# Attention maxima carried within SBUF, split in four operations, with another order at the start of each attention pair

## Chip, cores and metric

One core of one Trainium2 chip runs the whole program. The metric is the device time of one execution in microseconds, the median of several runs. Times inside an execution come from one profiled execution and count from its span's start.

## The reference

Four sequences of 512 tokens, 128 wide, go through six residual layers. Two are half-weighted attention over routed feed-forward projections (`_L0_ffn_ref`), two half-weighted mixtures of experts, one a state-space layer. The change touches only the causal multi-head attention between the two feed-forward layers:

```
q, k = rope(x @ wq.T), rope(x @ wk.T)           # 16 heads of 8
v    = x @ wv.T
scores = einsum('bhqd,bhkd->bhqk', q, k) / sqrt(8)
scores = scores + slopes[h] * (key position - query position)
scores = where(later key, -1e9, scores)
out = softmax(scores) @ v                       # softmax over keys
x = x + out @ out_w.T + out_b
```

## The kernel before

Everything is kept in SBUF; one program with five instruction streams (TensorE, VectorE, ScalarE, GpSimd and the DMA queue SP) that meet at semaphores. The sequences go in two pairs; each pair runs all six layers, and a layer's two sequences are two units. The attention of a pair is thus two units, one behind the other with a common plan, and stands at 131 to 250 us for the first pair and at 777 to 896 us for the second.

**What an attention unit does.** The 16 heads are four quads of four. In a first pass TensorE makes all scores in the order query by key ("slots", L1828 with the mask L1830, 11 slots to a quad, 44 to a unit), and VectorE reduces each to the negated row maximum (L1428). When the 11 slots of a quad are done, `max_parts` splits the float32 maxima into three bfloat16 parts. The job "turn" transposes these parts on TensorE to 12 rows (L1554, cbf with a_mp), ScalarE copies them to the tile a_mT (L1016), and SP brings them into three extra rows of each head's query operand a_qs, so that the maximum is subtracted within the product of the second pass. In that second pass TensorE makes the scores key by query (L1760, masks L1763 and L1765), ScalarE takes the exponential into a_p (L999), and TensorE weighs the values with it (L1789, `weigh_heads`).

**The plan.** The second pass has 32 steps for a unit (8 to a quad), 64 to a pair. `heads_plan()` writes the order of the other jobs by hand: the list at -1 runs before step 0, the others behind the scores of their step. The first unit's slots and turns go at 1.5 jobs a step until they are used up; `NEXT_MAXIMA` says in which steps the second unit's are taken; "vals" are the value projections, "rows" the transposes of finished heads, "ctr" and "out" the output projection. Step 8q of a unit waits for the maxima of quad q (L1754). All engines walk the same plan.

**Banks.** Jobs before number `RING_OF_4` (the length of the list at -1, less 3) use four PSUM banks in turn; later ones use two. `bank_free` makes TensorE wait for the reader of the job before in that bank, in the ring of two that of the second job before. The scores use the other banks.

**The next unit's preparation.** `hand_over(u, i)` runs stage i of the next unit: on VectorE 0 is the statistics of X (L1159 to L1178), 2 the Newton step (L1153 to L1155) and the normalised rows (L1188); the exponent guess of GpSimd stands between them (L773). Then follow the transposes, projections, rotations (L1405, L1409) and residuals (L1414) of queries and keys, and their bfloat16 parts by ScalarE (L906).

**SP's queue, in program order, for the first unit of a pair.** Quad 0: wait for a_mT, transfers. Quad 1: the same, then `head_rows(k + 1, 0)`, the second unit's query parts to stack_dram (L609, six transfers). Quad 2: wait for a_mT, transfers, then `head_rows(k + 1, 1)`, the key parts (L609, six). Quad 3: wait for step 15, `head_rows_in(k + 1, 0)` and `(k + 1, 1)`, which load a_q (L616) and a_k (L620) from stack_dram for the second unit's first slots; then wait for a_mT and transfers. Here "transfers" are one write of a_mT to max_dram (L708), a wait until it has landed, and two reads into a_qs (L712).

Of the kernel before, what the change touches and what calls it, by code (L numbers as in the profile page):

```python
# [8 lines left out]
BF16 = mybir.dt.bfloat16  # L9
# [4 lines left out]
P = 128  # L14
# [37 lines left out]
def heads_plan():  # L52


    def maxima(x):
        jobs = [("slot", x, n) for n in range(QUADS * NS1)]
        for quad in range(QUADS):

            jobs.insert((quad + 1) * NS1 + quad + 2, ("turn", x, quad))
        return jobs  # L60

    plan = {step: [] for step in range(-1, 2 * NS2 + 1)}
    first, second = maxima(0), maxima(1)
    plan[-1] = first[:NS1] + [("vals", 0, 0)] + first[NS1:NS1 + 8]
    first = first[NS1 + 8:]
    for step in range(2 * NS2):
        count = int(1.5 * (step + 1)) - int(1.5 * step)
        plan[step] += first[:count]
        first = first[count:]
        if step == NEXT_VALUES:  # L70
            plan[step].append(("vals", 1, 0))
        for start, stop, count in NEXT_MAXIMA:
            if start <= step < stop:
                number = int(count * (step + 1)) - int(count * step)
                plan[step] += second[:number]
                second = second[number:]
        x, quad = divmod(step // STEPS_4 - 1, QUADS)
        if step % STEPS_4 == 5 and step > STEPS_4:
            plan[step].append(("rows", x, quad))
        if step == NS2 + 7:  # L80
            plan[step].append(("ctr", 0, 0))
        if step == NS2 + 9:
            plan[step].append(("out", 0, 0))
    plan[2 * NS2] = [("rows", 1, QUADS - 1), ("ctr", 1, 0), ("out", 1, 0)]
    assert not first and not second
    return plan


NEXT_VALUES = 12
NEXT_MAXIMA = [(19, 51, 1.5)]  # L90
HEADS_PLAN = heads_plan()


# [80 lines left out]
def program(nc, A, out):  # L174
    with ExitStack() as ctx:
# [121 lines left out]
        a_o = sb("a_o", [P, T], F32, s)  # L297
        a_mx = sb("a_mx", [P, QUADS, NT, 4], F32, s)
        a_mr = sb("a_mr", [P, NT, 4], F32, s)
        a_mp = sb("a_mp", [P, QUADS, NT, 3, 4], BF16, s)  # L300
        a_rec = sb("a_rec", [P, NT, 4], F32, s)

        sb("f_end", [P, 352], F32, s)
# [45 lines left out]
        stack_dram = nc.dram_tensor("stack_dram", [2, 2, P // 2, HEADS // 2, T], BF16, kind="Internal").ap()  # L349
        comb_dram = nc.dram_tensor("comb_dram", [2, EXPERTS, T], F32, kind="Internal").ap()  # L350
        c_dram = nc.dram_tensor("c_dram", [2 * NSTATE, T], F32, kind="Internal").ap()
        max_dram = nc.dram_tensor("max_dram", [QUADS, 12, T], BF16, kind="Internal").ap()


        signals = []
# [93 lines left out]
        a_mpt = sig("a_mpt", "mha", QUADS)  # L449
        a_mtr = sig("a_mtr", "mha", QUADS)  # L450
        a_mok = sig("a_mok", "mha", QUADS)
        a_mwr = sig("a_mwr", "mha", QUADS, 16)
        a_mld = [sig(f"a_mld_{n}", "mha", 2, 16) for n in range(QUADS)]
        a_s2 = sig("a_s2", "mha", NS2)
        a_e2 = sig("a_e2", "mha", NS2)
        a_pv = sig("a_pv", "mha", 4 * NT)
# [128 lines left out]
        def _(sp):  # L585
# [104 lines left out]
            for u, (kind, p) in enumerate(UNITS):  # L690
                k = kth[u]
                if kind == "mha":
                    if p == 0:

                        sp.wait_ge(unit_done, done_before(u))
                        head_rows_in(k, 2)
                        head_rows_in(k, 3)
                    for quad in range(QUADS):
                        if p == 0 and quad == 3:

                            sp.wait_ge(a_s2.sem, a_s2.at(k, NS2 // 2 - 1))
                            head_rows_in(k + 1, 0)
                            head_rows_in(k + 1, 1)
                        sp.wait_ge(a_mok.sem, a_mok.at(k, quad))
                        if p == 1:

                            sp.wait_ge(a_mld[quad].sem, a_mld[quad].at(k - 1, 1))
                        a_mwr.by(sp.dma_start(max_dram[quad], a_mT))  # L708
                        sp.wait_ge(a_mwr.sem, a_mwr.at(k, quad))
                        for odd in range(2):  # L710
                            r = 64 * odd + MAX_ROW
                            a_mld[quad].by(sp.dma_start(a_qs[quad // 2][r:r + 3, 2 * (quad % 2):2 * (quad % 2) + 2],  # L712
                                                  max_dram[quad].rearrange("(c h o) t -> o c h t", c=3, o=2)[odd]))
                        if p == 0 and quad in (1, 2):
                            head_rows(k + 1, quad - 1)
                        if p == 0 and quad == QUADS - 1:

                            sp.wait_ge(a_s2.sem, a_s2.at(k, 3 * STEPS_4 - 1))
                            head_rows_in(k + 1, 2)
                        if p == 1 and quad == 0:  # L720

                            sp.wait_ge(a_s2.sem, a_s2.at(k - 1, NS2 - 1))
                            head_rows_in(k, 3)
                if kind == "ffn" and u + 1 < NU and UNITS[u + 1][0] == "mha":
                    k = kth[u + 1]
                    a_rld.by(sp.dma_start(rope[:], A["rope"]))
                    head_rows(k, 0)
                    if k == 0:
                        sp.wait_ge(rows_in, 64)
                        sp.wait_ge(w_lo.sem, w_lo.at(0, len(SPLITS) - 1))  # L730
                    head_rows(k, 1)
                    head_rows_in(k, 0)
                    head_rows_in(k, 1)
                if kind == "mamba":
                    state_rows(k)
                if u + 1 < NU and UNITS[u + 1][0] == "moe":
                    combine_rows(kth[u + 1], 1 - p)
                if kind == "moe" and u % PER_PAIR >= PER_PAIR - 2:
                    if p == 1:
                        for n in range(2):  # L740

                            sp.wait_ge(m_res.sem, m_res.at(k - 1 + n, 0))
                            b = batch_of(u - 1 + n)
                            load(out[b].rearrange("t p d -> p t d"), X[:, b], x_out)
# [104 lines left out]
        def _(act):  # L849
# [159 lines left out]
            def head_job(k, job, n):  # L1009
                b = job_bank(HEADS_JOBS.index((job, k % 2, n)))  # L1010
                if job == "turn":
                    act.wait_ge(a_mtr.sem, a_mtr.at(k, n))
                    if n >= 1 or k % 2 == 1:

                        act.wait_ge(a_mwr.sem, a_mwr.at(k, n - 1))
                    a_mok.by(act.activation(a_mT, bank[0:12, b, 0:T // 2].bitcast(BF16), ACT.Copy))  # L1016
                if job == "vals":
                    act.wait_ge(a_vpr.sem, a_vpr.at(k, 0))
                    if k % 2 == 1:

                        act.wait_ge(a_vok.sem, a_vok.at(k - 1, 1))
                    a_vst.by(act.activation(flat(a_vs[:]), bank[:, b, :], ACT.Copy))
                if job == "ctr":
                    act.wait_ge(a_ctr.sem, a_ctr.at(k, 0))
                    a_cok.by(act.activation(a_o[:], bank[:, b, :], ACT.Copy))
# [86 lines left out]
        def _(dve):  # L1112
# [254 lines left out]
            def mha(u, k, p):  # L1367

                b = batch_of(u)
                if p == 0:  # L1370
                    for n, (job, x, which) in enumerate(HEADS_PLAN[-1]):
                        head_job(k, job, which, b)
                        if n == NS1 - 1:
                            hand_over(u, 0)
                        if n == NS1 + 3:
                            hand_over(u, 2)
                    hand_over(u, 6)
                V.tensor_tensor(X[:, b], X[:, b], out_b[:].unsqueeze(1).to_broadcast([P, NT, P]), ALU.add)
                for s_ in range(NS2):
                    for job, x, which in HEADS_PLAN[NS2 * p + s_]:  # L1380
                        head_job(k - p + x, job, which, b - p + x)
                    if s_ >= HEAD_LAG[p] and s_ >= 1:
                        hand_over(u, s_ - HEAD_LAG[p])
# [47 lines left out]

            def max_parts(k, quad):
                dve.wait_ge(a_m1.sem, a_m1.at(k, quad * NS1 + NS1 - 1))
                step(V.tensor_copy(a_mp[:, quad, :, 0, :], a_mx[:, quad]))
                step(V.tensor_tensor(a_mr[:], a_mx[:, quad], a_mp[:, quad, :, 0, :], ALU.subtract))
                step(V.tensor_copy(a_mp[:, quad, :, 1, :], a_mr[:]))
                step(V.tensor_tensor(a_mx[:, quad], a_mr[:], a_mp[:, quad, :, 1, :], ALU.subtract))
                a_mpt.by(V.tensor_copy(a_mp[:, quad, :, 2, :], a_mx[:, quad]))

            def own_rows(p, b):  # L1440

# [97 lines left out]
        def _(pe):  # L1539
# [201 lines left out]
            def mha(u, k, p):  # L1741
# [5 lines left out]
                for s_ in range(NS2 + 3 * p):  # L1747
                    at = NS2 * p + s_
                    if s_ < NS2:
                        g, kt, pair = s_ // (2 * NT), s_ // 2 % NT, s_ % 2  # L1750
                        w = T - kt * P
                        if s_ % STEPS_4 == 0:

                            pe.wait_ge(a_mld[g].sem, a_mld[g].at(k, 1))  # L1754
                        if at >= 2:
                            pe.wait_ge(a_e2.sem, a_e2.at(k, s_ - 2))
                        scores, shared = score_pair(s_), kt >= NT // 2
# [354 lines left out]
```

## Time and profile before

| | us |
|---|---|
| median of 3 runs (lowest, highest) | 1321.04 (1320.27, 1321.16) |
| the profiled execution | 1319.3 |
| its span | 1317.5 |
| TensorE busy in the span | 1218.0 (92%) |
| VectorE busy | 906.7 (69%) |
| ScalarE busy | 641.4 (49%) |
| GpSimd busy | 241.4 (18%) |
| mean granted clock of TensorE | 0.992 of full |

The span is the time from the first to the last instruction of the profiled execution; the execution's own time is 1.8 us longer. Times of the rows are starts within the span.

### The profile page before, as it was taken

The page shows a single profiled execution, that of the slowest core. Times are in us where ns is not written, and L with a number is a line of the kernel's source. Part 1 is how long each engine was busy: PE and PEld are TensorE (multiplying, and loading weights), DVE is VectorE, ACT ScalarE, POOL GpSimd, SP SyncE. Part 2 cuts the span into 40 slices and gives each one's busy share as a digit, 9 for nine tenths or more (in the row PEclk, how much of TensorE's full clock was granted, in tenths as well). Part 3 has the DMA queues.
Part 4 walks back from the last instruction along what each step waited for, and adds up shares of the span by engine and source line. Part 5 has one row for each costly group of instructions (what it writes and reads, how often), then busy time and mean ns, then how long its engine had stood idle before and what let it go on. Part 6 is the DMA issues. An engine that isn't in the chain of part 4 may idle for free.

```text
span 1317.5 us, 17189 instructions
## 1 busy us (share of the span) xinstructions
PE 1218.0 (92%) x6083; PEld 784.5 (60%) x6132; DVE 906.7 (69%) x1754; ACT 641.4 (49%) x1188; POOL 241.4 (18%) x205
## 2 busy tenths in 40 slices
PE   5998788899899989899999969889998998999998
PEld 3676444567666555556667744446776664555665
DVE  6765867455467698986765667665455677889765
ACT  4544354543422597952235425554443227979222
POOL 3000100000020084751000010000000102938210
PEclk9999899999999999999999999999999999999999
DMA  7212130000101030320200031200002011212120
GB/s 232 57 33 79 49 85 19 2 1 1 65 1 65 10 113 20 118 81 0 73 25 1 17 97 48 70 3 0 1 1 65 27 39 61 78 58 80 65 73 9
DMA packets 34069, 63.27 MB, mean 48 GB/s; under 512 B 4576, under 2 KB 20288, under 8 KB 33792
## 3 DMA queue, kind: packets, MB, share of 16 engines
q1 hardware_dynamic: 33984, 62.17, 15.1%
q8 instruction: 49, 0.80, 0.3%
q14 instruction: 36, 0.29, 0.1%
HBM read 54.23 MB, written 8.45 MB: 48 GB/s over the span
## 4 chain that ended last, share of the span: by engine, by line
PE 73%; DVE 11%; ACT 9%; issue 3%; POOL 2%; DMA 1%; SPq 1%; another core or an unknown queue 0%; DVEq 0%; POOLq 0%; ACTq 0%
PE bank L1545 14%; PE bank L1546 13%; PE bank L1547 13%; PE bank L1724 9%; PE bank L1554 5%; DVE a_mx L1428 3%; ACT n_part L1095 3%; PE bank L1879 3%; PE bank L1623 3%; ACT n_da L1087 2%; PE bank L1694 2%; PE bank L1789 2%; POOL n_hc L842 2%; PE bank L1760 2%; PE bank L1828 1%
## 5 line engine op out<-in xcount | busy, mean ns | idle before, releaser
L1272 DVE SCALAR_TENSOR_TENSOR f_hl<-bank,f_hh 128x512 fp32r<-128x512 f32 x192 | 131.9, 689 | 130.9 <-ACT f_hh L916 130.1
L916 ACT ACTIVATE f_hh<-bank 128x512 fp32r<-128x512 f32 x192 | 114.9, 598 | 188.6 <-PE bank L1623 149.8
L982 ACT ACTIVATE m_sl<-bank 128x512 f32<-128x512 f32 x144 | 86.2, 599 | 235.2 <-PE bank L1547 234.8
L842 POOL TENSOR_TENSOR n_hc<-n_h,n_cs 128x512 f32<-128x512 f32 x128 | 160.7, 1283 | 35.7 <-DVE n_h L1516 31.4
L1545 PE MATMUL bank<-xT_h,mw_h 128*128 128x512 f32 x288 | 161.2, 560 | 3.5 <-DVEq L537 2.7
L1516 DVE TENSOR_TENSOR_SCAN n_h<-n_da,bank 128x512 f32<-128x512 f32 x128 | 149.2, 1205 | 5.3 <-PE bank L1554 2.5
L1724 PE MATMUL bank<-m_h,mw 128*128 128x512 f32 x288 | 145.6, 594 | 0.0
L1339 DVE TENSOR_TENSOR m_t<-m_sl,bank 128x512 f32<-128x512 f32 x128 | 87.9, 687 | 78.8 <-PE bank L1547 77.7
L773 POOL TENSOR_TENSOR small<-small,half 128x4 f32<-128x4 f32 (+1 forms) x24 | 26.8, 1117 | 577.7 <-DVE small L1178 577.7
L1879 PE MATMUL bank<-n_hc,ident 128*128 128x512 f32 x256 | 130.9, 599 | 0.2
L1428 DVE TENSOR_REDUCE a_mx<-bank 128x1 f32<-128x384 f32 (+3 forms) x176 | 105.9, 637 | 34.0 <-PE bank L1830 31.8
L999 ACT ACTIVATE a_p<-bank 128x1024 f32<-128x1024 f32 (+3 forms) x128 | 88.0, 704 | 79.8 <-PE bank L1765 42.9
L1545 PE MATMUL bank<-f_hh,fw_h 128*128 128x512 f32 x192 | 109.9, 572 | 6.1 <-DVE f_hl L1272 6.1
L1547 PE MATMUL bank<-xT_h,mw_l 128*128 128x512 f32 x288 | 114.6, 398 | 0.0
L1546 PE MATMUL bank<-xT_l,mw_h 128*128 128x512 f32 x288 | 114.2, 396 | 0.0
L1554 PEld LDWEIGHTS bank<-ident,n_part 128*128 128x128 f32 x480 | 56.4, 142 | 77.6 <-issue 44.8
L1095 ACT ACTIVATE n_part<-bank,n_bT 128x256 f32<-128x256 f32 x240 | 99.7, 578 | 3.4 <-PE bank L1554 3.4
L1087 ACT ACTIVATE n_da<-n_dt,amat 128x512 f32<-128x512 f32 x128 | 93.0, 824 | 5.2 <-DVE n_dt L1501 3.8
L1554 PE MATMUL bank<-ident,n_part 128*128 128x128 f32 x480 | 74.1, 280 | 14.5 <-ACT n_part L1095 12.8
L1545 PE MATMUL bank<-xT_h,fw_h 128*128 128x512 f32 x192 | 83.2, 434 | 0.9 <-POOL b1w L755 0.9
L1347 DVE TENSOR_TENSOR m_h<-m_t,m_c 128x512 f32<-128x512 f32 x112 | 77.5, 692 | 3.9
L1545 PEld LDWEIGHTS bank<-xT_h,mw_h 128*128 128x128 f32 x288 | 54.6, 190 | 38.9 <-issue 28.7
(248 smaller groups left out, 2335.4 us busy)
## 6 DMA issues: line engine op xcount, KB each, us to landing
n_cs<-c_dram SPq DMA_DIRECT2D x32, 512.0 KB, 3.7
m_c<-comb_dram SPq DMA_DIRECT2D x28, 512.0 KB, 5.0
a_q<-stack_dram SPq DMA_DIRECT2D x16, 256.0 KB, 3.6
a_k<-stack_dram SPq DMA_DIRECT2D x32, 128.0 KB, 3.5
stage_fw<-in_fw_dram SPq DMA_DIRECT2D x6, 512.0 KB, 7.0
stack_dram<-R SPq DMA_DIRECT2D x16, 192.0 KB, 2.9
w_stage<-in_mw_dram SPq DMA_DIRECT2D x9, 256.0 KB, 2.7
stack_dram<-R SPq DMA_DIRECT2D x16, 128.0 KB, 2.6
```

Source lines behind the costliest of these rows:

```text
L842: n_hcs.by(nc.gpsimd.tensor_tensor(n_hc[:, i % 4, :], n_h[:, i % 4, :], n_cs[:, j % C_RING, i // 2 % 2, :], ALU.mult))
L1087: n_das.by(act.activation(n_da[:, i % 4, :], n_dt[:, i % 2, :], ACT.Exp, scale=amat[:, i % 2, i // 2:i // 2 + 1]))
L1095: ins = act.activation(n_sx[p][:, n % 2, c, :], dtx_rows(c), ACT.Copy, scale=n_bT[:, c, n:n + 1])
L1272: f_lo.by(V.scalar_tensor_tensor(f_h[1][:, i % 4, :], bank[:, i % 3, :], 0.0, f_h[0][:, i % 4, :].bitcast(F32), ALU.max, ALU.subtract))
L1428: a_m1.by(V.tensor_reduce(a_mx[:, quad, qt, h0:h0 + nh], src, AX_X, ALU.max, negate=True))
L1516: n_scan.by(V.tensor_tensor_scan(n_h[:, i % 4, :], n_da[:, i % 4, :], drive(i), 0.0, ALU.mult, ALU.add))
L1545: mm(dst, w[0], x[0], start=start, stop=False)
L1546: mm(dst, w[0], x[1], start=False, stop=False)
L1547: return mm(dst, w[1], x[0], start=False, stop=stop)
L1554: ins = nc.tensor.transpose(dst(t), src(t), idn)
L1724: m_s2.by(mm(bank[:, 6, :], mw2[:, e, m, :], m_h[:, i2 % 3, :], start=i2 == 0, stop=i2 == MSTEPS - 1))
L1879: n_ya.by(mm(bank[:, 2 + i % 2, :], ident[:], n_hc[:, i % 4, :], start=i < 2, stop=i >= 2 * NSTATE - 2))
```

## The change

Five edits, all in the attention pair.

1. The transfer of the maxima: max_dram, its write and the wait for it go. SP sends each head's three rows straight from a_mT to a_qs, four transfers for a quad. ScalarE's next copy to a_mT now waits for those four of the quad before.
2. `max_parts` makes the parts in four operations, the parts of one head now lying side by side in a_mp.
3. VectorE's statistics of the second unit (stage 0) run before the first maximum of the pair, and stage 2 runs behind the 11th job and no longer behind the 15th.
4. The list at -1 holds five jobs of the first unit behind "vals", not eight.
5. The second unit's maxima are taken in steps 20 to 51, not 19 to 50.

```diff
-    plan[-1] = first[:NS1] + [("vals", 0, 0)] + first[NS1:NS1 + 8]
-    first = first[NS1 + 8:]
+    plan[-1] = first[:NS1] + [("vals", 0, 0)] + first[NS1:NS1 + 5]
+    first = first[NS1 + 5:]
...
-NEXT_MAXIMA = [(19, 51, 1.5)]
+NEXT_MAXIMA = [(20, 52, 1.5)]
...
-        a_mp = sb("a_mp", [P, QUADS, NT, 3, 4], BF16, s)
+        a_mp = sb("a_mp", [P, QUADS, NT, 4, 3], BF16, s)
...
-        a_mwr = sig("a_mwr", "mha", QUADS, 16)
-        a_mld = [sig(f"a_mld_{n}", "mha", 2, 16) for n in range(QUADS)]
+        a_mld = [sig(f"a_mld_{n}", "mha", 4, 16) for n in range(QUADS)]
...
                         sp.wait_ge(a_mok.sem, a_mok.at(k, quad))
-                        if p == 1:
-                            sp.wait_ge(a_mld[quad].sem, a_mld[quad].at(k - 1, 1))
-                        a_mwr.by(sp.dma_start(max_dram[quad], a_mT))
-                        sp.wait_ge(a_mwr.sem, a_mwr.at(k, quad))
-                        for odd in range(2):
-                            r = 64 * odd + MAX_ROW
-                            a_mld[quad].by(sp.dma_start(a_qs[quad // 2][r:r + 3, 2 * (quad % 2):2 * (quad % 2) + 2],
-                                                  max_dram[quad].rearrange("(c h o) t -> o c h t", c=3, o=2)[odd]))
+                        for h in range(4):
+                            r = 64 * (h % 2) + MAX_ROW
+                            a_mld[quad].by(sp.dma_start(a_qs[quad // 2][r:r + 3, 2 * (quad % 2) + h // 2],
+                                                        a_mT[3 * h:3 * h + 3]))
...
-                    if n >= 1 or k % 2 == 1:
-                        act.wait_ge(a_mwr.sem, a_mwr.at(k, n - 1))
+                    if n >= 1:
+                        act.wait_ge(a_mld[n - 1].sem, a_mld[n - 1].at(k, 3))
+                    elif k % 2 == 1:
+                        act.wait_ge(a_mld[QUADS - 1].sem, a_mld[QUADS - 1].at(k - 1, 3))
...
                 if p == 0:
+                    hand_over(u, 0)
                     for n, (job, x, which) in enumerate(HEADS_PLAN[-1]):
                         head_job(k, job, which, b)
                         if n == NS1 - 1:
-                            hand_over(u, 0)
-                        if n == NS1 + 3:
                             hand_over(u, 2)
...
-                step(V.tensor_copy(a_mp[:, quad, :, 0, :], a_mx[:, quad]))
-                step(V.tensor_tensor(a_mr[:], a_mx[:, quad], a_mp[:, quad, :, 0, :], ALU.subtract))
-                step(V.tensor_copy(a_mp[:, quad, :, 1, :], a_mr[:]))
-                step(V.tensor_tensor(a_mx[:, quad], a_mr[:], a_mp[:, quad, :, 1, :], ALU.subtract))
-                a_mpt.by(V.tensor_copy(a_mp[:, quad, :, 2, :], a_mx[:, quad]))
+                first, second, third = (a_mp[:, quad, :, :, c] for c in range(3))
+                step(V.tensor_copy(first, a_mx[:, quad]))
+                V.tensor_tensor(a_mr[:], a_mx[:, quad], first, ALU.subtract)
+                step(V.tensor_tensor(second, a_mx[:, quad], first, ALU.subtract))
+                a_mpt.by(V.tensor_tensor(third, a_mr[:], second, ALU.subtract))
...
-                            pe.wait_ge(a_mld[g].sem, a_mld[g].at(k, 1))
+                            pe.wait_ge(a_mld[g].sem, a_mld[g].at(k, 3))
```

## Rows read from the trace of the kernel before

**Rows 1.** Page, chain that ended last: share of the span by line.

```profile
PE bank L1545 14%; PE bank L1546 13%; PE bank L1547 13%; PE bank L1724 9%; PE bank L1554 5%; DVE a_mx L1428 3%; ACT n_part L1095 3%; PE bank L1879 3%; PE bank L1623 3%; ACT n_da L1087 2%; PE bank L1694 2%; PE bank L1789 2%; POOL n_hc L842 2%; PE bank L1760 2%; PE bank L1828 1%
```

**Rows 2.** Windows: A:B, length, busy PE PEld DVE ACT POOL, clock, DMA share, GB/s.

```profile
131.00:148.00 17.00, 10.11 (x66) 5.59 (x67) 15.13 (x43) 1.18 (x2) 4.99 (x6) 0.88 0.30 77
148.00:248.00 100.00, 87.21 (x738) 44.24 (x743) 67.19 (x154) 55.80 (x88) 1.81 (x3) 0.99 0.15 40
145.00:151.00 6.00, 5.10 (x21) 2.74 (x23) 4.37 (x8) 1.71 (x3) 0.00 (x0) 0.51 0.00 1
794.00:894.00 100.00, 86.59 (x742) 43.77 (x748) 66.88 (x154) 55.20 (x87) 1.81 (x3) 0.99 0.16 40
```

**Rows 3.** Timeline of VectorE, 131 to 148: start, duration, operation, count, idle before.

```profile
133.11 6.14 DVE L1428 TENSOR_REDUCE a_mx<-bank 128x4 f32<-128x512 f32 x11 [0.83 <-PE bank L1830]
139.28 0.17 DVE L1434 CAST a_mp<-a_mx 128x16 bf16<-128x16 f32 x1
...
140.12 0.17 DVE L1438 CAST a_mp<-a_mx 128x16 bf16<-128x16 f32 x1
140.20 0.86 DVE L1159 BATCH_NORM_STATS2 st<-X 128x6 f32<-128x128 f32 x4
...
141.59 1.28 DVE L1428 TENSOR_REDUCE a_mx<-bank 128x4 f32<-128x512 f32 x2
142.89 0.36 DVE L1153 SCALAR_TENSOR_TENSOR small<-small 128x4 f32<-128x4 f32 x1
...
144.75 1.15 DVE L1428 TENSOR_REDUCE a_mx<-bank 128x2 f32<-128x512 f32 x2
```

**Rows 4.** Timeline of TensorE, 139 to 149: first turn, two slots, first scores.

```profile
140.44 0.38 PE L1554 MATMUL bank<-cbf,a_mp 128*12 128x128 bf16 x4 [0.59 <-DVE a_mp L1438]
...
142.34 0.34 PE L1828 MATMUL bank<-a_k,a_q 128*128 128x384 bf16 x1 [1.08 <-DVE a_mx L1428]
...
145.49 0.50 PE L1828 MATMUL bank<-a_k,a_q 128*128 128x384 bf16 x1 [2.77 <-DVE a_mx L1428]
...
148.01 0.63 PE L1760 MATMUL bank<-a_q,a_k 128*128 128x512 bf16 x1
```

**Rows 5.** Timeline of SP's queue, 156 to 183; the a_q tile's idle row.

```profile
157.65 0.31 SPq L708 DMA_DIRECT2D max_dram<-R  x1
159.02 1.43 SPq L712 DMA_DIRECT2D a_q<-max_dram  x2
...
170.43 0.33 SPq L708 DMA_DIRECT2D max_dram<-R  x1
...
173.73 3.90 SPq L609 DMA_DIRECT2D stack_dram<-R  x6
...
  DMA a_q<-max_dram: 0.4, 1
```

**Rows 6.** Timeline of TensorE: steps 8, 13, 14, 22, 30, the last turn.

```profile
162.40 0.22 PE L1763 MATMUL bank<-cbf 128*128 128x128 bf16 x1 [0.16 <-issue]
...
173.70 0.66 PE L1554 MATMUL bank<-ident,a_o 128*128 128x128 f32 x4 [1.45 <-DVE a_mx L1428]
...
175.08 0.29 PE L1760 MATMUL bank<-a_q,a_k 128*128 128x128 bf16 x2
...
188.61 0.28 PE L1760 MATMUL bank<-a_q,a_k 128*128 128x128 bf16 x2
...
200.27 0.29 PE L1760 MATMUL bank<-a_q,a_k 128*128 128x128 bf16 x2
...
233.18 0.38 PE L1554 MATMUL bank<-cbf,a_mp 128*12 128x128 bf16 x4 [1.20 <-DVE a_mp L1438]
```

**Rows 7.** Chain of waits, 177 to 184: start, duration; the wait from TensorE's timeline.

```profile
177.03 2.07 DMA stack_dram<-R
...
179.79 3.38 DMA a_k<-stack_dram
...
183.31 0.38 PE L1828 MATMUL bank<-a_k,a_q 128*128 128x128 bf16 x4 [0.38 <-DMA a_k<-stack_dram]
```

More of the change, by code:

```diff
@@ L351, in program @@
         c_dram = nc.dram_tensor("c_dram", [2 * NSTATE, T], F32, kind="Internal").ap()
-        max_dram = nc.dram_tensor("max_dram", [QUADS, 12, T], BF16, kind="Internal").ap()
         signals = []
```

## Prediction

> **What bounds the kernel now.** I read the chain of work first. Matrix products of the feed-forward, expert and state layers carry it, and no line of them is touched; of what is touched only the maxima stand high in it, with 3% [rows 1]. So the windows of the two attention stretches come next. One begins at 131 and one at 777; the 100 us of steps of both have the same busy times to within 1% [rows 2], so everything is worked out for the first and doubled. Its head, before the first scores, lasts 17 us with VectorE busy for 15.13 and TensorE for 10.11 at a granted clock of 0.88. The 100 us behind it, with the 64 steps, have TensorE busy for 87.21 and VectorE for 67.19 [rows 2]. The head is thus VectorE's, the steps are mostly TensorE's, and any wait that holds TensorE inside a step is paid.
>
> In the head the timeline of VectorE shows no gap but 0.83 us at its start [rows 3]. TensorE stands still beside it for 2.77 us at a time and starts its first scores at 148.01 [rows 4]. In the steps two transfers show through already: TensorE waited 0.4 us for the maxima of the second quad at step 8 [rows 5], and 0.38 us for the keys of the second unit at 183.31 [rows 7]. The chain of waits between 177 and 183 is made of nothing but the way of those keys: issues on SP, landing in DRAM, landing back in SBUF [rows 7]. Both are at the edge of being late, which is why I follow them and not the busy shares.
>
> **Part 1, the statistics in front of the maxima.** They go from 140.20 to 141.59, 1.4 us with their last small operation, and the first maximum starts at 133.11 after 0.83 us without work [rows 3]. Put first, they start when the barrier opens, at 132.4, and end at 133.85. The maxima move by +0.75, what follows them gains 1.4, and 0.65 is won on VectorE. They will run beside GpSimd's fills of 132 to 136. The one small operation that the trace shows beside GpSimd took 0.36, twice the 0.17 of operations of its size [rows 3]; so a meeting costs 0 to 0.3 us here. I take 0, since no row shows statistics slowed.
>
> **Part 2, the parts in four steps.** Five operations start 0.21 apart (139.28 to 140.12 in four spacings) [rows 3]; one of them goes, 0.2 us for each of 8 quads. The strided writes have 16 elements to a partition as before: 0 extra, at most the 0.2 that is won. A fifth of a microsecond is paid only where TensorE waits for a turn.
>
> **Part 3, the newton step and the normalised rows** now stand behind the 11th maximum and no longer behind the 13th. That is 142.89 to 144.75, 1.9 us [rows 3]. It moves ahead of two maxima, and there is a catch: with five jobs ahead the ring of four banks ends at job 14, so the first turn uses a bank of the ring of two and waits for the maximum two jobs before it, the 12th. Before, it ran at 140.44 right behind the parts [rows 4]. Now: maxima 133.85 to 140.0, parts to 140.75, rows to 142.6, 12th maximum to 143.25, turn at 143.3, copy done at 144.3 (transposes 0.4, copy 0.6).
>
> **Part 4, the transfer of the maxima.** Before, from copy's end to step 8's scores: the write is issued at 157.65, the first read at 159.02, so the write has landed after 1.37 us; the two reads are 0.7 apart, and the scores wait until 162.2, 2.45 after the last read's start [rows 5, 6]. Together 4.55. Now four transfers of three rows. No row has one inside SBUF. Nearest is the write to DRAM, issue 0.31 and landing 1.37: three spacings of 0.38 and 1.37 make 2.5 us. The dear end is the spacing and landing of the reads, 0.8 and 2.45: 4.9 us. I take 2.5, for the form is that of the write (plain rows, SBUF as source) and no DRAM is read. So 2.05 us are saved for each quad, at 8 quads, wherever somebody waits for it. SP issues 1.5 us for a quad now.
>
> The write of this trace landed in 1.37 [rows 5]. The Trainium skill (DMA: Bandwidth & Descriptors, "Anatomy of one DMA — SWDGE (gpsimd) path") gives a transfer of GpSimd's path a fixed cost of about 2.0 us, most of it the receipt of the last write, heaviest where the target is HBM. The trace is below the figure, so the measurement goes ahead; by the page each landing below would come 0.6 later, at two places a pair that carry on, and the sum would be an estimated 2.4 us higher.
>
> First scores: after the copy at 144.3 the rows land at 146.8. TensorE has done its other jobs by 145.75 (two slots and the next unit's transposes instead of five slots). It starts at 146.8 instead of 148.01: **-1.2 us**. With the dear transfer it is 149.2, +1.2.
>
> **Part 5, five jobs ahead and not eight.** The 64 steps hold three more jobs; steps 0 to 18 hold as many as before, but each three places earlier in the list. I list the plan of both: the first unit's turns go from steps 4, 12, 19 to 6, 14, 21, and are needed at 8, 16, 24. The second unit's maxima start at step 20, its turns go from 27, 35, 43, 50 to 29, 37, 45, 51, needed at 32, 40, 48, 56.
>
> Step 8: turn 1 runs one projection, two slots and one weighing before it. I get its copy done 12.9 us after the first scores, the landing at 15.4, TensorE ready at 14.5; before, step 8 came after 14.2. **+1.2 us.** Then the first unit's quad 2: the steps up to 14 need what they needed, 12.9 us in the old trace (162.2 to 175.08) [rows 6], less 0.2 for the shorter parts. Turn 2 stood in step 12 and SP had it at 170.43 [rows 5]; in step 14 its copy ends 1.4 behind that step's start. 146.8 + 15.4 + 12.7 + 1.4 = 176.3. TensorE, ready for step 16 after 0.95, waits 1.6 for the landing.
>
> **SP's queue is the point.** Behind turn 2's transfer SP holds the six writes of the second unit's keys. Before, the turn was long past and they began at 173.73, as soon as ScalarE had the last part [rows 5]. Now SP stands in its wait for turn 2 until 176.3, issues four transfers until 177.8, and only then the six. From their start to the second unit's first slot are 183.31 - 173.73 = 9.6 us [rows 5, 7]. So that slot comes at **187.4**, in step 20. TensorE would be there 2.6 us earlier, and waits. Behind it in steps 20 and 21: the slot, scores, the turn with its wait for the bank, two slots, rows, weighing, 3.75 us with the durations of the timeline. Step 22 starts at 191.15; before, at 188.61 [rows 6]: **+2.5 us**, in which the -1.2 of the head is contained.
>
> From step 22 to 50 the pattern of eight steps took 11.66 us (188.61 to 200.27) [rows 6]; with the turn behind a weighing its wait for VectorE shrinks, but the rows job behind the turn waits for the turn's copy: 11.6. **-0.2** for three quads. At the end turn 3 stands directly behind the last slot (steps 50, 51); it waited 1.20 us for the parts at 233.18 [rows 6] and waits some 1.8, a step later. That is +1.3 at step 51, of which the last steps, where TensorE is not full, give back about half: **+0.7**.
>
> Sum: 2.5 - 0.2 + 0.7 = +3.0 a pair, +6 for both. The profiled run has 1319.3 us (1317.5 span, 1.8 around it); 1325.3 by its account. The median of the runs shown lies 1.7 above it: **1327**.
>
> **What could add or take away.** TensorE's clock was 0.51 of full between 145 and 151, its level of 1.2 GHz, after standing for 2.77 us; a product of 384 columns took 0.34 us before and 0.50 in it, the first of 512 columns 0.63 [rows 2, 4]. If the new head, whose idle pieces lie elsewhere, keeps the clock up, 1.5 us a pair are won (2.9 us of scores at half speed). If the wait of 2.6 us at step 20 pulls it down, about the same is lost. I take neither.
>
> **Rivals.**
> (a) The jobs are not late. If steps 0 to 14 run denser than I think, since VectorE has lost 0.65 us in the head and 0.2 for each quad and TensorE's waits for it go, turn 2 comes before 174 and SP is not held. Then -1.2 for the head, -1.6 for eight shorter parts, up to -1.5 for the clock, +1.3 for step 51: about -2.5 a pair, 1316. It decides at the old 173.73 minus the 1.5 of SP's four issues: turn 2's copy must end by 172.2. Against it: vals and the wait for the key parts lie between steps 12 and 14, and TensorE stood 1.45 us there [rows 6] for reasons that the change leaves.
> (b) Held, but made up: the wait at step 20 fills the banks and the exponentials, and the steps behind it catch up by 2 to 3 us: within 2.6 us of 1321.
> (c) The four transfers are dear (4.9 us). First scores +1.2, step 8 another 2.4 later, turn 2 at 181, the second unit's first slot at 194 and step 22 at +9; steps 32, 40 and 48 wait some 1.5 each: 14 us a pair, 1349. For it: the two reads wrote into these same rows, and took 0.7 each to issue [rows 5].
> (d) The change does not do what it says: the turn's wait for the bank, not the transfer, sets the first scores, and the head gains nothing: 1329.4, a case of the forecast.
>
> **Chances.** Forecast with (d) 0.52; (a) 0.26; (b) 0.16; (c) 0.06. About 0.2%, 2.6 us, is what a measurement can tell from no change. Faster 0.27, same 0.18, slower 0.55. The range takes (a) in without the gain of the clock at its best, and on the other side a fallen clock at step 20 with landings 0.6 later: 1315.5 to 1332.5. The forecast's own range is 1324 to 1332.
>
> **What would show it.** First scores at 146.8, held by the DMA of a_q; the first turn 2.5 us or more behind the parts; L609's second group of six starting behind turn 2's four issues, near 177.8, and TensorE waiting 2 us or more for a_k in step 20; a wait of 1 to 2 us for a_q at steps 8 and 16; step 22 near 191. Wrong it is if the six writes start before 175, or if the four transfers land more than 1 us off 2.5.

## The result and the profile after

| | before | after |
|---|---|---|
| median of the runs, us | 1320.79 | 1341.41 (1338.88, 1341.41, 1343.81) |
| ratio, 95% interval | | 1.0159 (1.0142 to 1.0176) |
| profiled execution, its span | 1319.3, 1317.5 | 1338.88, 1337.1 |
| forecast | | 1327.0 (1315.5 to 1332.5) |

A fourth execution of the changed kernel took 3120 us, a disturbance, and is left out; with it in the sample the median would read 1342.61. The change makes the kernel slower by 20.6 us. The forecast said slower too, by some 6 us; the measured time lies outside its range. Step numbers, "turn" and "slot" are those of the plan; R is the tile of which a_mT is a part, and the views name it in place of a_mT.

The page of the changed kernel first: the header, the costliest group that names what is waited for (line, operation, forms; busy us and mean ns; idle time before it and its releaser), and from the view of waits the totals for the span (us, times, longest).

```profile
span 1337.1 us, 17228 instructions
L1754 PE MATMUL bank<-a_q,a_k 128*128 128x512 bf16 (+3 forms) x256 | 64.3, 319 | 17.5 <-DMA a_q<-R 16.9
PE bank L1754 <- DMA a_q<-R: 16.9, 8, 3.1
```

TensorE stands 16.9 us, at eight steps, for the maxima's rows on their way within SBUF. Before, the same view had no such row for its products, and 0.8 us at two of its weight loads. Not all of the 16.9 is loss: 6.0 of it lie in front of the first scores of the two pairs, which start only 0.3 to 0.4 us later than before. The other waits, some 11 us, are the larger part of the 20.6. The pairs agree: 10.3 us of the loss fall into the first (the next layer begins at 258.68 and began at 248.41), and the second is 10.2 longer from its first slot to the next layer (126.98 and 116.77).

VectorE's timeline in the head, which answers [rows 3] (start, duration, operation, count, idle before):

```profile
132.33 0.87 DVE L1154 BATCH_NORM_STATS2 st<-X 128x6 f32<-128x128 f32 x4
...
133.65 0.63 DVE L1173 TENSOR_SCALAR small<-mv 128x4 f32<-128x4 f32 x1
133.73 6.13 DVE L1422 TENSOR_REDUCE a_mx<-bank 128x4 f32<-128x512 f32 x11
139.89 0.18 DVE L1429 CAST a_mp<-a_mx 128x16 bf16<-128x16 f32 x1
...
140.50 0.47 DVE L1148 SCALAR_TENSOR_TENSOR small<-small 128x4 f32<-128x4 f32 x1
...
142.47 1.28 DVE L1422 TENSOR_REDUCE a_mx<-bank 128x4 f32<-128x512 f32 x2
```

The head went as forecast to within 0.25 us: statistics from 132.33 (132.4), maxima done at 139.86 (140.0), rows behind the parts. The last small operation of the statistics took 0.63 us beside GpSimd's fills, and 0.17 without them before. That is more than the 0 to 0.3 that a meeting was given, though the maxima end on time. TensorE, answering [rows 4, 6 and 7]:

```profile
143.20 0.39 PE L1548 MATMUL bank<-cbf,a_mp 128*12 128x128 bf16 x4 [2.75 <-DVE a_mx L1422]
...
148.36 0.61 PE L1754 MATMUL bank<-a_q,a_k 128*128 128x512 bf16 x1 [2.85 <-DMA a_q<-R]
...
165.28 0.61 PE L1754 MATMUL bank<-a_q,a_k 128*128 128x512 bf16 x1 [2.20 <-DMA a_q<-R]
...
179.01 0.28 PE L1754 MATMUL bank<-a_q,a_k 128*128 128x128 bf16 x2
...
184.30 0.39 PE L1754 MATMUL bank<-a_q,a_k 128*128 128x512 bf16 x1 [2.93 <-DMA a_q<-R]
...
193.07 0.38 PE L1822 MATMUL bank<-a_k,a_q 128*128 128x128 bf16 x4 [1.30 <-DMA a_k<-stack_dram]
...
197.11 0.29 PE L1754 MATMUL bank<-a_q,a_k 128*128 128x128 bf16 x2
```

These are the first turn, then the scores of steps 0, 8, 14 and 16, the second unit's first slot, and step 22. Every wait that the forecast named is there, at its place and by its releaser. Those for a_q are longer than forecast (2.20 for 0.9 at step 8, 2.93 for 1.6 at step 16); the one for the keys at the second unit's first slot is shorter (1.30 for 2.6), for TensorE came there late itself. Against the kernel before the loss is 0.35 at step 0, 3.1 at step 8, 7.0 at step 16 and 8.5 at step 22 (188.61 before). SP's queue shows why, answering [rows 5]:

```profile
164.93 3.97 SPq L607 DMA_DIRECT2D stack_dram<-R  x6
180.37 2.81 SPq L705 DMA_DIRECT2D a_q<-R  x4
183.50 3.95 SPq L607 DMA_DIRECT2D stack_dram<-R  x6
...
188.95 1.30 SPq L618 DMA_DIRECT2D a_k<-stack_dram  x2
```

Turn 2's four issues take 2.81 us, 0.7 each, and the six key writes stand right behind them. The chain of waits shows one transfer whole, from ScalarE's copy to the scores:

```profile
143.63 0.60 ACT R L1011
144.24 0.86 SPq L705
145.10 0.05 issue
145.15 0.72 SPq L705
145.87 0.04 issue
145.91 0.64 SPq L705
146.55 0.05 issue
146.60 1.71 DMA a_q<-R
148.31 0.05 issue
148.36 0.61 PE bank L1754
```

From the copy's end, 144.24, to the scores: 4.12 us. The forecast had 2.5 from three spacings of 0.38 and a landing of 1.37; the spacings are 0.91, 0.76 and 0.69, and the landing, from the start of the fourth issue, is 1.71. Last, two windows of 6 us behind waits of TensorE (busy PE, PEld, DVE, ACT, POOL, then the granted clock):

```profile
165.00:171.00 6.00, 5.69 (x34) 3.02 (x35) 3.01 (x6) 2.66 (x3) 0.00 (x0) 0.72 0.51 134
184.00:190.00 6.00, 5.70 (x37) 2.77 (x37) 2.58 (x5) 3.60 (x5) 0.00 (x0) 0.72 0.65 162
```

The mean of 0.72 over six microseconds means that TensorE spent part of them at 1.2 GHz: here a wait of 2.2 or 2.9 us is paid a second time in the clock.

### The profile page after: what moved, and what is told of

Read it like the earlier page. It is cut to its first block, busy times and chain, and to the rows that moved or that the text cites. A ratio compares the mean times of both kernels' runs of the same rounds, so it can differ in the third digit from the quotient of the medians.

```text
span 1337.1 us, 17228 instructions
## 1 busy us (share of the span) xinstructions
PE 1224.2 (92%) x6132; PEld 784.2 (59%) x6132; DVE 903.5 (68%) x1738; ACT 640.5 (48%) x1188; POOL 241.8 (18%) x205
## 4 chain that ended last, share of the span: by engine, by line
PE 71%; DVE 11%; ACT 9%; issue 3%; POOL 2%; SPq 2%; DMA 2%; DVEq 0%; POOLq 0%; ACTq 0%
PE bank L1539 13%; PE bank L1540 13%; PE bank L1541 13%; PE bank L1718 9%; PE bank L1548 5%; ACT n_part L1090 3%; PE bank L1617 3%; PE bank L1873 3%; DVE a_mx L1422 3%; ACT n_da L1082 2%; PE bank L1688 2%; PE bank L1783 2%; PE bank L1754 2%; POOL n_hc L835 2%; PE bank L1822 1%
## 5 line engine op out<-in xcount | busy, mean ns | idle before, releaser
L1822 PE MATMUL bank<-a_k,a_q 128*128 128x128 bf16 (+3 forms) x256 | 65.2, 313 | 17.9 <-DVE a_mx L1422 10.1
L1754 PE MATMUL bank<-a_q,a_k 128*128 128x512 bf16 (+3 forms) x256 | 64.3, 319 | 17.5 <-DMA a_q<-R 16.9
```

## The experiments

The code cuts show each edit in outline. Two theories. **Price**: the late transfer is dear, and nothing else failed in the sum. **Plan**: five jobs ahead instead of eight bring the turns late to steps 8 and 16, and that alone would have cost more than the forecast gave it. The kernel before, run beside them, had medians of 1319.45 to 1320.49.

**The transfer by way of DRAM, all else as changed (e1_dram).**

```
-  for h in range(4): a_qs rows <- a_mT[3h:3h+3]
+  max_dram[quad] <- a_mT;  wait;  two reads "(h o c) t -> o c h t" into a_qs
```

> The changed kernel with only the transfer of the maxima put back: one write to DRAM and two reads, all else as changed (five jobs ahead, second unit's maxima from step 20, statistics in front, four part operations). Theory A, the turns stand too late: the way from the copy's end to the scores was 4.55 us through DRAM and is 4.12 us within SBUF, so nothing much comes back: 1341 to 1347, with waits of 2 to 3 us for a_q at steps 0, 8 and 16. Rival B, the loss is in the four transfers within SBUF: 1321 to 1327, the old median and what the other edits cost.

Measured: 1331.14 us (1330.01 to 1332.69), ratio 1.0089 (1.0074 to 1.0104), between what the two theories gave. So the transfer within SBUF costs about 10 us against the way by DRAM, and a loss of about 10 more is left with that way too. Its chain:

```profile
144.02 1.35 DMA max_dram<-R
145.38 0.02 issue
145.39 0.27 SPq L712
145.66 0.04 issue
145.70 1.42 DMA a_q<-max_dram
147.13 0.05 issue
147.17 0.61 PE bank L1759
```

3.16 us by way of DRAM, a full microsecond less than within SBUF, and 1.4 less than the 4.55 of the kernel before: with the three parts of a head side by side the two reads are issued 0.3 apart in place of 0.7, and land sooner. So the change gave up a way that one of its own edits had made cheap. The two traces differ by 1.19 us at step 0 (148.36 and 147.17), 1.8 at step 8, 3.2 at step 14 and 4.0 at steps 16 and 22. The step from 1.8 to 3.2 holds no transfer: behind step 8 the changed kernel's clock has the 0.72 above, this one, after a wait of 1.51, reads 1.00 over six microseconds.

**Two of the four transfers (e3_two).** Half of the maxima aren't delivered here.

```
-  for h in range(4):
+  for h in range(2):
```

> The changed kernel with only two of the four transfers of each quad (the rows of the other two heads are left as they were, so half of the maxima don't arrive). From the copy's end to the scores one spacing of 0.7 and a landing of 1.7 remain: 2.4 us, which is what my forecast had priced for all four (2.5). If the forecast failed by this price alone, the time is 1325 to 1330 (forecast 1327), first scores near 146.8 and the second unit's first slot near 187.4. If it failed elsewhere too (the plan costs more than I summed), it stays above 1332.

Measured: 1330.57 us (1330.19 to 1331.55), ratio 1.0085 (1.0070 to 1.0100). That is 0.6 above what was expected if the price alone had failed, and below the 1332 of the other case. From the copy's end to the scores are 2.72 us now, close to the 2.5 of the forecast, so this run sets its sum beside a trace. TensorE, steps 0, 8, 16, the second unit's first slot, step 22:

```profile
146.77 0.61 PE L1754 MATMUL bank<-a_q,a_k 128*128 128x512 bf16 x1 [1.20 <-DMA a_q<-R]
...
162.82 0.39 PE L1754 MATMUL bank<-a_q,a_k 128*128 128x512 bf16 x1 [0.84 <-DMA a_q<-R]
...
179.06 0.39 PE L1754 MATMUL bank<-a_q,a_k 128*128 128x512 bf16 x1 [1.54 <-DMA a_q<-R]
...
188.03 0.38 PE L1822 MATMUL bank<-a_k,a_q 128*128 128x128 bf16 x4 [2.84 <-DMA a_k<-stack_dram]
...
192.97 0.28 PE L1754 MATMUL bank<-a_q,a_k 128*128 128x128 bf16 x2
```

Forecast were 146.8, 162.2, a wait of 1.6, 187.4 with a wait of 2.6, and 191.15. Everything up to the slot is there within 0.65 us. Step 22 is 1.8 late, 0.6 of it inherited; behind the wait of 2.84 the clock fell to 0.72 again:

```profile
188.00:194.00 6.00, 5.93 (x40) 2.90 (x40) 3.00 (x6) 1.66 (x4) 0.00 (x0) 0.72 0.21 50
```

**Keys ahead of turn 2 in SP's queue (e11_two_keys_first)**, on top of e3_two.

```
+  if p == 0 and quad == 2: head_rows(k + 1, 1)
   sp.wait_ge(a_mok.sem, a_mok.at(k, quad))
   ...
-  if p == 0 and quad in (1, 2): head_rows(k + 1, quad - 1)
+  if p == 0 and quad == 1: head_rows(k + 1, 0)
```

> The kernel of the third run (the changed kernel with two of the four transfers a quad, half of the maxima not delivered) with one thing moved on SP's queue: the six writes of the second unit's keys stand before the wait for turn 2, no longer behind its transfers. Theory A, SP's queue holds the keys: the writes start at 173.8 instead of 178.3, the wait of 2.84 us at the second unit's first slot goes, and turn 2's rows come 1.3 later at step 16: 1325 to 1329 against 1330.6. Rival E, the writes wait for something else than turn 2: the slot stays at 188 and the time at 1330 or above.

Measured: 1329.57 us (1328.71 to 1329.74), ratio 1.0072 (1.0054 to 1.0090). The wait for the keys goes, as the theory said, and the wait for a_q at step 16 grows from 1.54 to 2.76, for turn 2's transfers now stand behind six issues of keys. The time falls by 1.0 us, less than the theory gave: a wait was passed on. Here SP's order of these two, by which the forecast set so much, mostly decides which of them TensorE waits for.

**Eight jobs ahead again: by DRAM (e4_old_plan_dram), within SBUF (e5_old_plan_sbuf), and by DRAM with the second unit from step 20 (e10_eight_from20).**

```
-    plan[-1] = first[:NS1] + [("vals", 0, 0)] + first[NS1:NS1 + 5]
+    plan[-1] = first[:NS1] + [("vals", 0, 0)] + first[NS1:NS1 + 8]
...
-NEXT_MAXIMA = [(20, 52, 1.5)]     (e4, e5)
+NEXT_MAXIMA = [(19, 51, 1.5)]
```

> The kernel before with statistics in front, the rows behind the 11th job and the four part operations, but with the old plan (eight jobs ahead, second unit from step 19) and the way through DRAM. Theory A: 0.6 us of the head and up to 0.2 us for each quad that TensorE waits for: 1316 to 1320. Rival C, these edits cost something too (rows ahead of two maxima): 1321 to 1323.

> The changed kernel with the old plan (eight jobs ahead, second unit's maxima from step 19) and all else of the change: four transfers within SBUF, four part operations, statistics in front. Theory A, the late turns are the loss and the transfers are hidden where the turns stand four steps ahead: 1316 to 1320, as the same kernel through DRAM (1316.8). Rival B, the four transfers cost wherever they stand: above 1325.

> The kernel of the fourth run (statistics in front, four part operations, DRAM, eight jobs ahead) with the second unit's maxima from step 20 and not 19. Against the first run (1331.1) it differs in the five or eight jobs ahead alone. Theory A, five jobs ahead are the loss, not the start at 20: 1313 to 1317, with no wait for a_k. Rival D, the start at 20 carries the loss: 1322 to 1331.

Measured: 1316.79 (1315.45 to 1320.90), ratio 0.9979 (0.9969 to 0.9989); 1317.03 (1315.47 to 1318.05), ratio 0.9979 (0.9969 to 0.9989); 1315.82 (1314.36 to 1317.03), ratio 0.9965 (0.9951 to 0.9978), the fastest of the study. All three came as their theories said. Three readings. By DRAM, five ahead against eight (e1_dram and e10_eight_from20) is 1.0089 against 0.9965, some 16 us. The later start of the second unit's maxima is no part of the loss (e10 against e4). And with eight ahead the dear transfer costs nothing: e5 equals e4, since the turns are early. TensorE's timeline of e10 from 144 to 200 has no wait for a DMA; these are steps 0, 16 and 22:

```profile
146.65 0.63 PE L1759 MATMUL bank<-a_q,a_k 128*128 128x512 bf16 x1
...
176.14 0.39 PE L1759 MATMUL bank<-a_q,a_k 128*128 128x512 bf16 x1
...
186.08 0.29 PE L1759 MATMUL bank<-a_q,a_k 128*128 128x128 bf16 x2
```

Step 22 stands at 186.08, against 188.61 before [rows 6] and 193.16 in e1_dram: 7 us a pair between the two plans.

**Is it the turns or the slots? The first unit's turns two places earlier in the list, about one step, five ahead kept, by DRAM (e12_five_turns_early) and within SBUF (e16_sbuf_turns_early).**

```
-  jobs.insert((quad + 1) * NS1 + quad + 2, ("turn", x, quad))
+  jobs.insert((quad + 1) * NS1 + quad + (2 if x else 0), ("turn", x, quad))
```

> The changed kernel with the transfer by way of DRAM (1331.1 us), five jobs ahead kept, but the first unit's turns stand directly behind the last slot of their quad instead of two jobs later, some one and a half steps earlier. Theory: what five jobs ahead cost (15.3 us against eight ahead) is that the turns come late to steps 8 and 16 and hold up SP's key writes behind turn 2. Then about half of it comes back, since the turn now waits for the parts of VectorE instead: 1322 to 1327, no wait of 1.4 us or more for a_q at steps 8 and 16. Rival: the three slots that moved into the steps cost by themselves, TensorE has no room for them there; then it stays at 1330 to 1332.

> The changed kernel as it is (transfers within SBUF, five jobs ahead) with the first unit's turns directly behind the last slot of their quad. The same edit with the transfer by way of DRAM gave 1318.1 us in place of 1331.1. Theory: the dear transfer is paid only because the turns are late, so with early turns most of its 11.5 us go as well: 1318 to 1323, waits for a_q at steps 8 and 16 below 1 us. Rival: its price is a cost of its own with five jobs ahead, paid at each turn and in SP's queue: about 1318 + 11, 1327 to 1331, with waits of 1 us or more at steps 8 and 16.

Measured: 1318.14 (1317.01 to 1321.90), ratio 0.9990 (0.9980 to 1.0000); and 1323.39 (1322.42 to 1324.49), ratio 1.0028 (1.0017 to 1.0038). Two places in a list give back 13.0 us by DRAM, more than the theory asked, and 18.0 within SBUF (17 by the two ratios), where the time lies 0.4 above the range that the theory gave and 3.6 below that of its rival. So five jobs ahead are not too few by themselves; the turns were too late for them. The edit does one thing more. The first turn is now job 12 and uses the ring of four banks again, so it no longer waits for the 12th maximum: it runs at 141.40 in e12 and at 142.98 in e1_dram, and the first scores come 1.4 us earlier (145.75 and 147.17). Of the 5.3 us won at step 22 (187.87 and 193.16) that is about a quarter. SP's queue in e12, turn 2 and the keys:

```profile
171.78 0.31 SPq L708 DMA_DIRECT2D max_dram<-R  x1
173.15 0.57 SPq L712 DMA_DIRECT2D a_q<-max_dram  x2
174.05 3.88 SPq L609 DMA_DIRECT2D stack_dram<-R  x6
```

In e1_dram the same write was issued at 177.15 and the six at 179.41. In e16 TensorE waits 1.45, 0.40 and nothing at steps 0, 8 and 16, where the changed kernel had 2.85, 2.20 and 2.93; the transfer keeps its 4.1 us, but most of it is hidden, and the second unit's slot comes at 183.70. The 5.3 us over e12 don't come from the first pair. Behind the slot's wait of 2.62 the clock of e16 read 0.72 from 184 to 190, where e12, after a wait of 2.12, read 1.00; that made step 22 0.9 later (188.75 and 187.87), but the next layers begin at 250.29 and 250.17. In the second pair they begin at 898.69 and 893.97. There e16 is 2.1 behind at step 14 (820.56 and 818.46), with a clock of 0.51 from 790 to 796 where e12 has 0.95, and 4.3 behind at step 22, with 0.72 once more behind a slot's wait of 2.81. The transfers themselves were waited for 0.5 us in e16's second head and 0.4 at its step 8. So what is left shows in the traces as clock rather than as waits; one trace of each can't tell how much of it the transfer brings about.

**The helpful edits alone: parts and layout (e8_parts), statistics (e7_stats), transfers (e2_sbuf_only)**, each on the kernel before.

```
e8:  parts in four operations, a_mp [P, QUADS, NT, 4, 3], reads "(h o c) t -> o c h t"
e7:  hand_over(u, 0) in front of the list, hand_over(u, 2) behind job NS1 - 1
e2:  four transfers from a_mT, five part operations, a_mp [P, QUADS, NT, 4, 3]
```

> The kernel before with the four part operations and their layout alone (head by head; the reads from DRAM then take three neighbouring rows for each head). Theory A: 0.2 us for each quad that TensorE waits for, some 3 turns a pair, and the wait of 0.4 us at step 8 gone because the reads are issued in 0.3 and not 0.7: 1318 to 1320. Rival: no change, 1320 to 1322.

> The kernel before with one edit alone: the second unit's statistics run ahead of the first maximum, the rest as before (Newton step and normalised rows behind the same job). Forecast's reasoning: 0.65 us of VectorE's head are won for each pair, and the first scores come that much earlier: 1319 to 1320.5. Rival: the statistics run beside GpSimd's fills and are slowed, or another wait ends the head; then no difference: 1320.5 to 1321.5.

> The kernel before with only the transfer changed to four pieces within SBUF (and the layout of the parts that it needs, still written in five operations). Theory A: the old plan asks for the rows 5.7 us behind the turn, 4.12 us are enough, so 1319 to 1322, and the wait of 0.4 us at step 8 is gone. Rival B: 8 us or more slower than before.

Measured: e8 1317.45 (1316.53 to 1318.50), ratio 0.9983 (0.9973 to 0.9993); e7 1318.37 (1315.50 to 1320.42), ratio 0.9984 (0.9975 to 0.9993); e2 1320.26 (1318.05 to 1325.22), ratio 1.0005 (0.9993 to 1.0018). e8 and e7 are worth some 2 us each, somewhat more than was expected of them; the transfers are worth nothing on the old plan. What is recorded of e7 as one edit is two: the rows (`hand_over(u, 2)`) move in front of two maxima as well, so its 2 us are not those of the statistics alone.

**A better version?** Nine (e15_nine) and ten (e14_ten) jobs ahead in e10, and e10 with turns directly behind the last slot (e17_eight_turns_early).

> The same with nine jobs ahead. Theory that eight is about the best: 1315.5 to 1317. Rival that more ahead is better, since each slot that leaves the steps frees TensorE there: 1313.5 to 1315.2.

> The fastest version so far (parts in four steps, statistics in front, second unit's maxima from step 20, by way of DRAM, eight jobs ahead: 1315.8 us) with ten jobs ahead. Theory: with eight ahead no transfer is waited for in the steps of the first unit any more, so two more jobs ahead only lengthen the head by some 1 us of maxima on VectorE, of which the steps give part back: 1316 to 1318.5. Rival: TensorE stands in the head anyway and takes them for nothing, and the turns come earlier still: 1313 to 1315.5.

> The fastest version so far (parts in four steps, statistics in front, second unit's maxima from step 20, by way of DRAM, eight jobs ahead: 1315.8 us) with the first unit's turns directly behind their last slot. Theory: with eight ahead no turn was late, so there is nothing to win, and TensorE waits for VectorE's parts at the turns: 1316 to 1319. Rival: SP's key writes still come earlier and the second unit's first slots with them: 1313 to 1315.

Measured: 1317.95 (1316.33 to 1319.65), ratio 0.9985 (0.9976 to 0.9994); 1322.11 (1319.47 to 1324.65), ratio 1.0016 (1.0006 to 1.0025); 1318.88 (1318.17 to 1321.12), ratio 0.9995 (0.9986 to 1.0005). Nine and ten ahead were both worse than either side expected. The trace of ten has a clock of 0.72 from 172 to 178, where e10 reads 1.00; why ten costs 6 us was not taken apart further. Where the turns are early enough, moving them further ahead costs about 3 us: turns 1 and 2 of e17 wait 1.18 each for VectorE's parts, those of e10 for nothing. Eight ahead with the turns where they were is the best tried.

## Why the prediction was right in sign and wrong in size

**Right.** The bound (waits of TensorE inside steps), the head within VectorE, the turn's wait for the bank (2.75 us at 143.20), step 8 and step 16 waiting for a_q, SP held by turn 2 with the key writes behind, and 9.6 us from those writes to the slot: 193.07 - 183.50 = 9.57. Its own sign of being wrong, transfers more than 1 us off 2.5, came true. e3_two shows the sum itself within 0.65 us up to the slot at the price it assumed.

**The step that failed is Part 4, the transfer's price.** 2.5 us were taken, between ends of 2.5 and 4.9; measured are 4.12 at step 0, 3.81 at step 8 (copy's end 161.47, scores 165.28) and 3.95 at step 16. The excess is in SP's spacing, 0.7 to 0.9 in place of 0.38, three times, and in a landing of 1.7 in place of 1.37. Why an issue takes 0.7 here, and 0.3 for the reads of the new layout, no run shows. The price was chosen by likeness of form (SBUF as source, plain rows). The forecast's own rows held the other witness, from SBUF too: the six writes of keys in 3.90 us, 0.65 each [rows 5]. The two ends were worked through, 1327 and 1349: 22 us for 2.4 us of price, or 9.2 for one. At 4.12 that gives 1327 + 1.62 x 9.2 = 1341.9; measured is 1341.4. The agreement is luck: rival (c) counted 4.5 us a pair for waits at steps 32, 40 and 48, of which the trace has one of 0.39 at 211.09, and the forecast left out the clock and mis-sized the end, which make up for it (below). Nor is the price passed on evenly. From 2.72 us (e3_two) to 3.16 (e1_dram) the time grows by 0.6, from there to 4.12 by 10.3. e3_two is 1.1 ahead of e1_dram at the slot (188.03 and 189.11) and only 0.2 at step 22, for its clock fell behind the slot, where e1_dram's read 1.00. Still, rival (c) had the right mechanism and 0.06 of the chances, where two rows out of three for issues spoke for it, and the range stopped 16 us short of it.

**Its size in places, first pair**: step 0 late by 1.56 against the forecast, step 8 by 3.1 in all (162.2), turn 2's copy end by 4.1 (176.3), the key writes by 5.7 (177.8), the slot by 5.7 (187.4), step 22 by 6.0 (191.15), the pair's end by 7.3 (+10.3 in place of +3.0). The price is paid in series: 1.6 at step 0, 1.5 more at step 8, and 1.6 more in SP's four issues ahead of the keys. That is 4.7 of the 7.3. Another 1.0 is lost between step 8 and turn 2, 0.3 between the slot and step 22, and 1.3 at the end.

**Left out: the clock.** The forecast says: "If the wait of 2.6 us at step 20 pulls it down, about the same is lost. I take neither." In e3_two just that happened; in the changed kernel it fell behind steps 8 and 16. Between steps 8 and 14 the changed kernel took 13.73 us at a mean clock of 0.72 in the first six, e1_dram 12.35 at 1.00: 1.4 us. That is where the 1.0 ahead of turn 2 is lost. The head of the changed kernel didn't keep the clock up either (0.72 from 148 to 154). What makes the clock fall is open. It isn't the wait alone: the same transpose in step 13, after the same wait of 1.45, took 1.03 us in e5_old_plan_sbuf (first line), with 0.72 from 172 to 178, and 0.66 in e10_eight_from20 (second line), with 1.00.

```profile
173.01 1.03 PE L1548 MATMUL bank<-ident,a_o 128*128 128x128 f32 x4 [1.45 <-DVE a_mx L1422]
172.61 0.66 PE L1553 MATMUL bank<-ident,a_o 128*128 128x128 f32 x4 [1.45 <-DVE a_mx L1427]
```

**Wrong: the end of the pair.** From step 22 to the next layer 61.57 us were taken (197.11 to 258.68), 59.80 before; forecast was +0.5, measured +1.8. TensorE's last turn waited 1.62 us for the parts, as forecast (1.8). The traces of the other runs take it apart. Step 22 and the next layer in e4_old_plan_dram, the next layer in e10_eight_from20, then a wait and the next layer in the changed kernel:

```profile
191.61 0.28 PE L1759 MATMUL bank<-a_q,a_k 128*128 128x128 bf16 x2
250.49 0.50 PE L1544 MATMUL bank<-xT_h,fw_h 128*128 128x512 f32 x1
...
247.23 0.50 PE L1544 MATMUL bank<-xT_h,fw_h 128*128 128x512 f32 x1
...
211.09 0.39 PE L1754 MATMUL bank<-a_q,a_k 128*128 128x512 bf16 x1 [0.39 <-DMA a_q<-R]
...
258.68 0.50 PE L1539 MATMUL bank<-xT_h,fw_h 128*128 128x512 f32 x1
```

e4 takes 58.88 and e10 61.15, and only the start of the second unit's maxima differs: work that leaves the steps before 22 is done behind them, +2.3. The shorter parts give back 0.9 (e8_parts takes 58.90; e2_sbuf_only, with the new layout and five operations, 59.85). The wait of 0.39 for the dear rows is nearly all of the rest. The forecast gave the later start no term of its own here, and the parts 0.2.

**The plan was costed too low as well.** Against the way of DRAM as the change's own layout made it (3.16 us), five ahead, with turns two jobs behind the last slot, cost 7 us a pair; the forecast had +3.0 for the whole change. It saw the reads only at the old layout's 4.55, and gave the layout nothing. Of e8's 2 us the stretch above puts 0.9 a pair down to the shorter parts, so the layout is left with little on the old plan.

**Rivals.** (a) needed turn 2's copy to end by 172.2; it ended at 180.36. (b) needed the steps behind 20 to catch up; they lost 1.8 more. (d) isn't so: the first scores were held by the DMA. (c) is taken up above.

**A page beside it.** The Trainium skill (DMA: Bandwidth & Descriptors, "Anatomy of one DMA — SWDGE (gpsimd) path") gives a small transfer of GpSimd's path about 2.0 us fixed, heaviest to HBM. On SP's queue the landings here are 1.35 into DRAM, 1.42 out of it and 1.71 within SBUF: below the figure each time, and the one that never touches HBM is the longest. Other transfers of this queue are above it: the reads of the old layout took 2.45, and the keys' way back, in larger pieces, 3.38 [rows 7].

## What to carry to other kernels

Between two rows that could price a new operation, look for all that share one property with it, and where they differ by a factor of two, carry the dear one through the plan before giving it a chance: several waits in series depended on this transfer, and 1.4 us of it were worth 10.8 us (4.12 against 2.72). A job's place in a written order can be worth more than its duration: two places of a transpose moved 13 to 18 us here, and a cheaper or dearer transfer showed only where the order had used up its slack. Before a way by DRAM is given up, see what the same change of layout makes of it.

## What the runs showed of the hardware

- A transfer of three rows of 1 KB within SBUF was issued in 0.64 to 0.86 us on SP's queue and landed 1.7 us after the start of the last of four issues; twelve rows of the same tile to DRAM were issued in 0.31 and landed after 1.35. Four small transfers within SBUF took longer (4.12 us) than a write and two reads through DRAM (3.16).
- The same two reads from DRAM took 0.7 us each to issue with the parts of a head four rows apart, 0.27 to 0.3 with them side by side.
- After waits of 2.20 and 2.93 us (changed kernel), 2.84 (e3_two) and 2.62 (e16_sbuf_turns_early) TensorE's granted clock read 0.72 over the next six microseconds. Shorter waits went either way: 2.14 (e1_dram, step 16) was followed by 0.72 and 2.12 (e12_five_turns_early, the second unit's first slot) by 1.00; 1.85 (e4_old_plan_dram, the slot) by 0.55 from 184 to 190; 1.45 in step 13 by 0.72 in e5_old_plan_sbuf and by 1.00 in e10_eight_from20; 1.54 (e3_two, step 16) by 1.00. What a wait costs beyond its length can't be told from its length alone.
